# Fewer, larger DMAs in a two-layer attention kernel, and the DMAs that spread the sums of y moved from SyncE to ScalarE

## The reference

```
x = x + attn_a(layernorm(x))     # 16 heads of 16, causal softmax, then weights times a decay table of lag (0 from lag 511 on)
x = x + ffn(layernorm(x))        # 256 -> 1024 -> 256, weights alpha * sign(w), exact gelu
x = x + attn_b(layernorm(x))     # 16 heads of 16, causal softmax, biases, layernorm with gamma and beta behind it
x = x + ffn(layernorm(x))
```

## Time and profile before

| | |
|---|---|
| median of 3 runs | 2720.69 us (2717.49 to 2722.33) |
| the profiled execution's own time | 2716.31 us |
| its span, first to last instruction | 2714.6 us |
| mean granted TensorE clock | 0.947 |
| busy: PE / DVE / ACT / POOL | 2399.4 / 1956.2 / 1497.6 / 1054.6 us |
| first DMA of qkv_a, att_a, mid, att_b, end (SP) | at 34.3, 157.4, 1155.3, 1499.9, 2462.6 us |

### The profile page before, as it was taken

The page is one execution under the profiler, slowest core; times in us unless marked ns, Lnnn a source line. Parts: engine busy times, 40 slices in busy tenths (PEclk is TensorE's granted clock), DMA queues, the critical chain, the costliest instruction groups (busy, mean ns, idle before and its releaser), DMA issues. The chain is left out here.

```text
span 2714.6 us, 44575 instructions
## 1 busy us (share of the span) xinstructions
PE 2399.4 (88%) x13600; PEld 1368.4 (50%) x13600; DVE 1956.2 (72%) x4832; ACT 1497.6 (55%) x3293; POOL 1054.6 (39%) x1274
## 2 busy tenths in 40 slices
PE   4959999999999999749996699999999999993788
PEld 2535545555554555337764355555555555542666
DVE  5568888878887877337663787878788787842887
ACT  1218687776867767514331166666666666671233
POOL 0037877788787778713211301010000101003552
PEclk8969999999999999969998699999999999996999
DMA  4995142342514230055546742351523425004210
GB/s 129 254 144 70 22 61 40 45 53 30 78 26 56 40 45 6 8 151 116 118 96 127 92 63 39 44 68 28 66 35 49 62 30 69 8 5 136 70 55 32
DMA packets 185947, 180.66 MB, mean 67 GB/s; under 512 B 90352, under 2 KB 122864, under 8 KB 184944
## 3 DMA queue, kind: packets, MB, share of 16 engines
q1 hardware_dynamic: 185712, 177.81, 37.6%
HBM read 114.37 MB, written 61.60 MB: 65 GB/s over the span
## 5 line engine op out<-in xcount | busy, mean ns | idle before, releaser
L703 POOL TENSOR_TENSOR att_a_wd<-att_a_wt,decay 128x256 f32<-128x256 f32 (+3 forms) x896 | 754.7, 876 | 212.8 <-PE att_a_po L874 122.4
L729 ACT ACTIVATE att_b_wt<-att_b_ps 128x512 f32<-128x512 f32 (+3 forms) x1280 | 591.8, 538 | 347.6 <-PE att_b_ps L852 345.5
L769 DVE TENSOR_REDUCE att_a_mpart<-att_a_pm 128x1 f32<-128x512 f32 x768 | 508.6, 685 | 117.1 <-PE att_a_pm L839 112.5
L769 DVE TENSOR_REDUCE att_b_mpart<-att_b_pm 128x1 f32<-128x512 f32 x768 | 502.6, 684 | 96.2 <-PE att_b_pm L839 94.7
L839 PE MATMUL att_a_pm<-att_a_kop,att_a_qop 128*128 128x512 f32 (+3 forms) x1280 | 511.9, 425 | 54.2 <-DMA att_a_qop<-att_a_qop 28.9
L729 ACT ACTIVATE att_a_wt<-att_a_ps 128x512 f32<-128x512 f32 (+3 forms) x896 | 432.4, 510 | 210.7 <-PE att_a_ps L855 148.0
L839 PE MATMUL att_b_pm<-att_b_kop,att_b_qop 128*128 128x512 f32 (+3 forms) x1280 | 487.7, 399 | 49.8 <-DMA att_b_qop<-att_b_qop 30.6
L852 PE MATMUL att_b_ps<-att_b_qop,att_b_kop 128*128 128x512 f32 (+3 forms) x1280 | 455.3, 385 | 13.0 <-DMA att_b_qop<-att_b_mrow 8.2
L713 POOL TENSOR_SCALAR_AFFINE_SELECT att_b_wt<-att_b_wt 128x512 f32<-128x512 f32 x128 | 81.6, 637 | 851.0 <-ACT att_b_wt L729 851.0
L839 PEld LDWEIGHTS att_a_pm<-att_a_kop,att_a_qop 128*128 128x128 f32 x1280 | 238.8, 194 | 317.4 <-DVE att_a_mpart L769 140.3
L839 PEld LDWEIGHTS att_b_pm<-att_b_kop,att_b_qop 128*128 128x128 f32 x1280 | 245.0, 194 | 267.8 <-DVE att_b_mpart L769 131.4
(11 more groups left out here) (165 smaller groups left out, 2500.6 us busy)
## 6 DMA issues: line engine op xcount, KB each, us to landing
att_a_kop<-qk SPq DMA_DIRECT2D x128, 128.0 KB, 6.4
att_a_qop<-qk SPq DMA_DIRECT2D x128, 128.0 KB, 7.0
att_b_kop<-qk SPq DMA_DIRECT2D x128, 128.0 KB, 6.3
att_b_qop<-qk SPq DMA_DIRECT2D x128, 128.0 KB, 6.7
qk<-qkv_a_qk_hi SPq DMA_DIRECT2D x32, 256.0 KB, 4.8
qk<-qkv_a_qk_lo SPq DMA_DIRECT2D x32, 256.0 KB, 4.5
qk<-mid_qk_hi SPq DMA_DIRECT2D x32, 256.0 KB, 4.2
qk<-mid_qk_lo SPq DMA_DIRECT2D x32, 256.0 KB, 4.6
```

The source lines that it names most:

```text
L703: pool.tensor_tensor(wd[:, kq % 2, j, a:z], wt[:, kq % buffers, j, a:z], keep["decay"][:, u:u + z - a], ALU.mult).then_inc(w_decayed, 1)
L729: act.activation(wt[:, kq % buffers, j, a:CH], pe_[:, n % EBANKS, 0:CH - a], ACT.Exp)\
L769: dve.tensor_reduce(mpart[:, c, piece, u:u + 1], pm[:, n % MBANKS, 0:w], AX.X, ALU.max, negate=True).then_inc(m_reduced, 1)
```

## The change

1. Stores of q and k: the DRAM tensor `qk` is laid out so that one DMA stores all of hi and one all of lo, in `projections` and in "mid" (2 DMAs in place of 8), and hi is stored without a wait for lo. `v` is laid out so that one DMA stores all heads (1 in place of 4); the attention loads v of a group with 4 DMAs, one per chunk, in pieces of 256 or 272 bytes, in place of one with pieces of four times that.
2. Attention, the sums: `y` is stored whole, all 128 partitions, by one DMA of 256 KB in place of 4 of 32 KB. The 4 DMAs that spread the sums are begun by ACT, which first waits for its own copy (`o_kept`) and for `s_ready` of the chunk two before. `scol`, `inverse`, `mneg` and `ftotal` use every second column or partition of 32, so that the transposed far sums `frow` are added directly and the 8 DMAs of "FT" with `fcol` are gone.
3. Attention, the start: ACT begins the 16 `qop` loads of group 0, SP the 16 `kop` loads. Groups 0 and 1 have no DMA that clears the row of `qop`.
4. Dense: `load_y` begins 4 DMAs of 256 KB (two for y, two for inverse) in place of 17. At the start ACT begins wp, x of chunk 0 and the sign matrices; bo, gamma and beta have a semaphore of their own; the wait for the q, k, v weights on DVE stands ahead of item ("X", 1).

```diff
-                sp.wait_ge(hi_ready, M * G + M)
-                sp.wait_ge(lo_ready, M * G + 2 * M)
-                for hl, t in ((0, qk_hi), (1, qk_lo)):
-                    for a in range(2):
-
-                        for qk in range(2):
-                            dst = dram["qk"][b, :, hl, qk, :, c * CH:(c + 1) * CH]
-                            dst = dst.rearrange("(m a) p t -> a p m t", a=2)[a]
-                            sp.dma_start(dst, t[64 * a:64 * a + 64, par, KT * qk:KT * qk + KT, :].bitcast(F32))\
-                              .then_inc(stored[par], 16)
+                for hl, t, ready, n in ((0, qk_hi, hi_ready, M * G + M), (1, qk_lo, lo_ready, M * G + 2 * M)):
+                    sp.wait_ge(ready, n)
+                    dst = dram["qk"][b, hl].rearrange("q (m a) p t -> (a p) (q m) t", a=2)
+                    sp.dma_start(dst[:, :, c * CH:(c + 1) * CH], t[:, par, :, :].bitcast(F32)).then_inc(stored[par], 16)
                 sp.wait_ge(v_kept, G + 2)
-                for gh in range(NG):
-                    sp.dma_start(dram["v"][b, gh, c][:, 0:TB * GH * VW].rearrange("p (t j e) -> p t j e", t=TB, j=GH),
-                                 vt[:, par, :, GH * gh:GH * gh + GH, :]).then_inc(stored[par], 16)
+                sp.dma_start(dram["v"][b, c][:, 0:TB * H * VW].rearrange("p (t h e) -> p t h e", t=TB, h=H),
+                             vt[:, par, :, :, :]).then_inc(stored[par], 16)
...
+                    if g:
+                        sp.dma_start(qop[rows, par, c, :, :].bitcast(F32), qk_g[g][r // 2, 0, :, :, cols])\
+                          .then_inc(qk_in[par][c], 16)
                 if g < 2:
-                    sp.wait_ge(q_padded[par], c + 1)
-                sp.dma_start(qop[MROW:MROW + 1, par, c, :, :].bitcast(F32),
-                             qop[96:97, par, c, :, :].bitcast(F32)).then_inc(qk_in[par][c], 16)
-                if c == NC - 1:
-                    sp.dma_start(va[:, par, :, :, :].rearrange("p (c t) j e -> p c (t j e)", c=NC), v_g[g])\
-                      .then_inc(v_in[par], 16)
+                    sp.sem_inc(qk_in[par][c], 16)
+                else:
+                    sp.dma_start(qop[MROW:MROW + 1, par, c, :, :].bitcast(F32),
+                                 qop[96:97, par, c, :, :].bitcast(F32)).then_inc(qk_in[par][c], 16)
+                for a in range(NC) if c == NC - 1 else ():
+                    sp.dma_start(va[:, par, TB * a:TB * (a + 1), :, :], v_g[g][a]).then_inc(v_in[par], 16)
...
                 if kind == "O":
                     c = item[2]
                     sp.wait_ge(o_kept, done(g, c) + 1)
-                    if done(g, c) > 2:
-                        sp.wait_ge(s_ready, done(g, c) - 2)
-                    for j in range(GH):
-                        h, cols = GH * (g % NG) + j, slice(c * CH, (c + 1) * CH)
-                        sp.dma_start(dram["y"][g // NG, h, :, cols], y[STRIP * j:STRIP * j + HD, c % 2, :])\
-                          .then_inc(y_out[c % 2], 16)
-                        sums = y[STRIP * j + HD:STRIP * j + HD + 1, c % 2, :].rearrange("o (i e) -> o i e", e=PIECE)
-                        sp.dma_start(scol[STRIP * j:STRIP * (j + 1), c % 2, :], sums).then_inc(s_in[c % 2], 16)
+                    sp.dma_start(dram["y"][g // NG, g % NG, :, c * CH:(c + 1) * CH], y[:, c % 2, :])\
+                      .then_inc(y_out[c % 2], 16)
...
         @block.scalar
         def _(act):
+            for c in range(NC):
+                for r in range(PAIRS):
+                    act.dma_start(qop[r * HD:(r + 1) * HD, 0, c, :, :].bitcast(F32),
+                                  qk_g[0][r // 2, 0, :, :, c * CH:(c + 1) * CH]).then_inc(qk_in[0][c], 16)
...
                     act.activation(y[:, c % 2, :], po[:, :], ACT.Copy).then_inc(o_kept, 1)
+                    act.wait_ge(o_kept, done(g, c) + 1)
+                    if done(g, c) > 2:
+                        act.wait_ge(s_ready, done(g, c) - 2)
+                    else:
+                        act.wait_ge(m_padded, 2)
+                    sums = y[HD:P:STRIP, c % 2, :].rearrange("j (t k i) -> j k t i", t=TB, k=P // SQUARE)
+                    for k in range(P // SQUARE):
+                        act.dma_start(scol[SQUARE * k:SQUARE * (k + 1):SPREAD, c % 2, :], sums[:, k, :, :])\
+                           .then_inc(s_in[c % 2], 16)
...
-                        dve.wait_ge(f_in[n], F_DMAS * (g + 1))
-                        dve.tensor_tensor(scol[:, c % 2, :], scol[:, c % 2, :], fcol[:, n, :], ALU.add).then_inc(s_summed, 1)
+                        dve.wait_ge(f_turned, TURNED[g, c])
+                        dve.tensor_tensor(scol[:, c % 2, :], scol[:, c % 2, :], frow[:, n, :], ALU.add).then_inc(s_summed, 1)
...
-                sp.dma_start(y[:, G % 2, :, :], dram["y"][b].rearrange("(k h) d t -> (h d) k t", k=KT)[:, :, cols])\
-                  .then_inc(y_in[G % 2], 16)
-                for h in range(H):
-                    part = slice(HD * (h % (H // KT)), HD * (h % (H // KT) + 1))
-                    sp.dma_start(inverse[part, G % 2, h // (H // KT), :],
-                                 dram["inverse"][b, h // GH, c, h % GH:h % GH + 1, :].to_broadcast([HD, CH])).then_inc(y_in[G % 2], 16)
+                rows = dram["y"][b].rearrange("g (j s) t -> (g j) s t", s=STRIP)
+                for k in range(KT):
+                    heads = slice(k * H // KT, (k + 1) * H // KT)
+                    sp.dma_start(y[:, G % 2, k, :], rows[heads, 0:HD, cols]).then_inc(y_in[G % 2], 16)
+                    sp.dma_start(inverse[:, G % 2, k, :],
+                                 dram["inverse"][b, c, heads, :].unsqueeze(1).to_broadcast([H // KT, HD, CH]))\
+                      .then_inc(y_in[G % 2], 16)
...
             load_y(0)
-            sp.dma_start(wp[:, :, :], w.rearrange("(t p) n -> p t n", p=P)).then_inc(w_in, 16)
-            load_x(0)
             if norm:
                 for t, src in zip((bo, gamma, beta), norm):
-                    sp.dma_start(t[:, :], row_of(src).to_broadcast([P, D])).then_inc(w_in, 16)
-            sp.dma_start(w1s[:, :, :].bitcast(F32), dram["w1s"]).then_inc(signs_in, 16)
-            sp.dma_start(w2s[:, :, :].bitcast(F32), dram["w2s"]).then_inc(signs_in, 16)
+                    sp.dma_start(t[:, :], row_of(src).to_broadcast([P, D])).then_inc(norm_in, 16)
             load_y(1)
...
+            act.dma_start(wp[:, :, :], w.rearrange("(t p) n -> p t n", p=P)).then_inc(w_in, 16)
+            act.dma_start(x[:, 0, :, :], at(x_src, 0, 0)).then_inc(x_in[0], 16)
+            act.dma_start(w1s[:, :, :].bitcast(F32), dram["w1s"]).then_inc(signs_in, 16)
+            act.dma_start(w2s[:, :, :].bitcast(F32), dram["w2s"]).then_inc(signs_in, 16)
...
-            if qkv:
-                dve.wait_ge(qkv_in, N_QKV)
-                dve.tensor_scalar(bqk[:, 0:KT], bqk[:, 0:KT], SCALE, None, ALU.mult)
-                dve.tensor_scalar(wqkv[:, :, 0:D], wqkv[:, :, 0:D], SCALE, None, ALU.mult).then_inc(w_scaled, 1)
-                dve.wait_ge(w_scaled, 1)
-                dve.wait_ge(vt_filled, 2)
-
             for item in PLAN:
                 G = item[1]
                 par = G % 2
+                if item == ("X", 1) and qkv:
+                    dve.wait_ge(qkv_in, N_QKV)
+                    dve.tensor_scalar(bqk[:, 0:KT], bqk[:, 0:KT], SCALE, None, ALU.mult)
+                    dve.tensor_scalar(wqkv[:, :, 0:D], wqkv[:, :, 0:D], SCALE, None, ALU.mult).then_inc(w_scaled, 1)
+                    dve.wait_ge(w_scaled, 1)
+                    dve.wait_ge(vt_filled, 2)
```

More of the change, by code:

```diff
@@ L554, in attention @@
             ftotal, frow = sb("ftotal", [P, NC - 2, SQUARE], F32), sb("frow", [P, NC - 2, SQUARE], F32)
-            fcol = sb("fcol", [P, NC - 2, PIECE], F32)
         y = sb("y", [P, 2, CH], F32)
-        scol, inverse = sb("scol", [P, 2, PIECE], F32), sb("inverse", [P, 2, PIECE], F32)
+        scol, inverse = sb("scol", [P, 2, SQUARE], F32), sb("inverse", [P, 2, SQUARE], F32)
         pm, pe_, po = ps("pm", [P, MBANKS, CH]), ps("ps", [P, EBANKS, CH]), ps("po", [P, CH])
@@ L575, in attention @@
         block = ctx.enter_context(nc.Block())
-        qk_g = dram["qk"].rearrange("b g h q (j d) t -> (b g) h q d j t", d=HD)
-        v_g = dram["v"].rearrange("b g c p e -> (b g) p c e")[:, :, :, 0:TB * GH * VW]
+        qk_g = dram["qk"].rearrange("b h q g (j d) t -> b g h q d j t", d=HD)
+        qk_g = [qk_g[g // NG, g % NG] for g in range(GROUPS)]
+        v_g = [[dram["v"][g // NG, c][:, 0:TB * H * VW].rearrange("p (t g e) -> g p t e", t=TB, g=NG)[g % NG]
+                .rearrange("p t (j e) -> p t j e", j=GH) for c in range(NC)] for g in range(GROUPS)]
         KBS = sum(len(near(c, decayed)) for c in range(NC))
@@ L656, in _ @@
                     for k in range(P // SQUARE):
-                        sp.dma_start(row[:, :, k, :], mrow[SQUARE * k:SQUARE * k + UNITS, c, :].bitcast(F32))\
```

(21 more changed lines are left out.)

64 lines of the change are left out of this document (28 added, 36 removed).

## The result

The changed kernel takes 2799.09 us (median of 4 runs, 2791.84 to 2803.77) where the kernel before takes 2720.65 (4 runs): the ratio is 1.0287 with a 95% interval of 1.0258 to 1.0317. It is slower, as forecast, but by 78 us and not by 18, and it lies above the range that was given.

A forecast was written before the change was run, and what follows sets the result against it. PE was taken to bound both attention stages. Gains of 60 us against 78 us of PE waits behind ACT's issues gave 18 us slower, 2734.3 for an execution like the profiled one, median 2739; range 2690 to 2775.

The forecast's parts named there:

- The loss: Both attentions: ACT stands about 2.2 us issuing DMAs at each O, PE waits 1.25 us per item, 78 us.
- rival C: Attentions: an occasional full queue or a PE clock dropping after stalls costs another 0.5 us per item, 2770; chance 0.08.
- Rival A: Attentions: ACT's stall is partly absorbed or its issues are shorter, so the kernel is faster, 2700 or 2671; chance 0.29.
- qkv_a, chunks and end: First projection: fewer SP issues save 2 us over 7 chunks, and att_a begins 3.5 us earlier.
- first load to first M, two attentions: Attention starts: the ninth DMA, which clears a row behind the others, goes; 2.5 us each, 5 us.
- ends of the attentions: Last spreading DMA begins some 2 us earlier, with four on ACT instead of eight on SP: 4 us for both.
- start of mid: No wait for `bv`; y, inverse and ACT's loads all arrive in 9.5 us, so PE starts 15.5 us earlier.
- mid after its first P: End of mid: with merged stores att_b begins at 1493.9 instead of 1499.9, 6 us.
- start of end: Same load sum as in mid gives a PE start at 2476 against 2478.95, 3 us.
- waits in att_b: Waits for `scol` and the row of maxima both go, 19 us, plus 2 us for lower clock: 21 us.
- Projections: qkv_a and mid: merged stores save 2 us in chunks, 3.5 us before att_a and 6 us before att_b.
- rival D: Dense starts: y loads with 8 heads outermost use half the DMA engines, 3 us each, 2745; chance 0.05.

The follow-up runs named there:

- e1: Changed kernel, but SyncE begins the four spreading DMAs again, behind its store of y: 2676.32 us, ratio 0.984.
- e4: Changed kernel, but ScalarE begins the four spreading DMAs one at a time, one behind each of its next four exponentials: 2677.8 us.
- e3: Changed kernel, but each of ScalarE's four spreading DMAs is cut in two, eight issues in a row: 3002.5 us.
- e2: Changed kernel, but ScalarE begins two of the four spreading DMAs and SyncE the other two: 2710.0 us.
- e10: e1 with the stores of qk and v cut into twelve DMAs a chunk again, in the new layouts: 2687.14 us, ratio 0.9892.
- e5: e1 with wp, x and the sign matrices begun by SyncE behind y, inverse and three rows, ahead of the second chunk's loads: 2666.1 us, ratio 0.9811.
- e11: e5 with y in its old DRAM layout, loaded by one DMA over 128 rows and stored by four at each O: 2665.1 us, ratio 0.9812.
- e9: e5 with the first chunk's y on SyncE and inverse on ScalarE, 8 DMAs each of outer dimension 16: 2671.7 us, ratio 0.9834.

## Why the prediction was right and wrong

The losses were sized at 78 us and measured at 125.9 (span of after less that of e1); the gains at 60 and measured at 38.5 (before less e1). The net is 87.4 us between the profiled executions, where 18 were forecast.

**The loss.** The mechanism was right: ACT's standstill, the banks, PE behind them in both stages, and nothing for it in att_a or att_b's slack. Its waits were sized right too: 1.23 us per item (76 us in all) against 1.25, behind a standstill of 2.38 us in the middle of the items against 2.2. The step that failed is that these waits were the whole loss. The PE clock was held at no loss, since it stood near 1.00 in steady groups with short waits, and matmuls that take longer behind a stall were in no term. They take 48 us longer in the two stages, 0.77 us per item, so that the loss is 2.00 us per item (1.98 by the medians) where 1.25 was forecast. The clock can have at most 43 of the 48 us; the rest stays open. A falling clock was one half of rival C, which got 0.08 and 0.5 us per item. Its other half, a queue that is now and then full, showed little: the longest issue in att_b is 0.59 us, and in att_a 3 of 128 are above 0.7 (1.27 the longest). So of the 69 us between forecast and result 48 are the longer matmuls, and 21.5 the gains that did not come.

The Trainium skill, page "DMA: Bandwidth & Descriptors", section "Issuing engines are not separate DMA queues", holds that spreading DMAs over engines saves only sequencer time, usually small beside the DMA itself. By e4 (1.5 us for all) that is so where the sequencer has room; by e3 (326 us) it is not, where an engine that feeds PE through three banks issues them in a row.

**Rival A** turned on a loss of 0.97 us per item, at a block of 1.9 us. On the line between e2 (1.25 us of block, 0.54 lost) and after (2.38, 1.98) that loss stands at 1.6 us. With gains of 38.5 us in place of 60 the sign turns at 0.62 us per item; e2 lies just below, and is just faster than before (2710.0 us, ratio 0.997, 0.9953 to 0.9986).

**The gains, one by one** (before against e1, and the same rows of e1):

| term | forecast | measured |
|---|---|---|
| qkv_a, chunks and end | 5.5 | 10.2 |
| first load to first M, two attentions | 5 | 3.9 |
| ends of the attentions | 4 | 2.9 |
| start of mid | 15.5 | 9.0 |
| mid after its first P | 6 | 8.9 |
| start of end | 3 | -3.2 |
| waits in att_b | 21 | 10.0 |
| att_a, end after its first P | 0 | -3.2 |

*Projections* were undersized: SP's issues, about half of the gain by e10, had held them back, and the bytes less than was taken. The last v is issued at 142.3 in e1 against 149.84 to 153.4, and its last 9.2 us move 284 GB/s at a share of 0.72, where 264 at a share of 1.01 had been taken for a limit of the engines.

*Starts of mid and end* were oversized by one step: "all 3.75 MB are in 9.5 us". The 395 GB/s of the earlier trace rows were the best of one stretch; in e1 the nine windows of 2 us from 1144 to 1162 move 151 to 348 GB/s. And y did not share the time evenly: it was complete last, 18.9 us after the first load. e5 puts the contention with ScalarE's 2.75 MB and SyncE's second chunk at 8.7 and 7.9 us for the two starts. e11 puts rival D at 2.2 and 2.1 us for the product, near its 2.5, with y alone changed and inverse still in 8 heads. The Trainium skill, the same page, section "Why a DMA increments its semaphore by 16 and not by 1", has 8 engines for an outer dimension of 8; the share of 0.62 in e5, where a half would be 0.50, agrees roughly. So the wait for `bv` did go, and half of the gain at mid went to a new wait; in end, where before loaded wp and the signs behind y, the change made the start slower.

*Waits in att_b* were oversized: DVE's waits for `scol` fell, and PE's behind it, but the wait for the row of maxima stayed, 6.6 us in 6 waits in e1 where before had 5.6 in 6. "MC's DMAs queue behind O's eight on SP" holds in a way: the DMAs of 13 of the 32 rows in before began 0.7 to 2.2 us behind their transposition. But PE waited for none of these. The 8 rows that it waited for began at once, as this one of before:

```profile
1613.74 0.21 DVE L809 STREAM_TRANSPOSE att_b_mrow<-att_b_mneg 128x32 f32<-128x32 f32 x1
1613.97 2.44 SPq L657 DMA_DIRECT2D att_b_qop<-att_b_mrow  x4
1617.60 0.50 PE L852 MATMUL att_b_ps<-att_b_qop,att_b_kop 128*128 128x512 f32 x1 [0.93 <-DMA att_b_qop<-att_b_mrow]
```

In e1 it is the same. The row's DMAs begin straight behind the transposition at 1690.94 (DVE and SP of e1), and the S matmul starts at 1694.82: the row's own 3.7 us are what PE waits for.

```profile
1690.94 0.20 DVE L799 STREAM_TRANSPOSE att_b_mrow<-att_b_mneg 128x32 f32<-128x32 f32 x1
...
1691.17 2.49 SPq L652 DMA_DIRECT2D att_b_qop<-att_b_mrow  x4
```

```profile
1694.82 0.50 PE L842 MATMUL att_b_ps<-att_b_qop,att_b_kop 128*128 128x512 f32 x1 [0.95 <-DMA att_b_qop<-att_b_mrow]
```

## What to carry to other kernels

A DMA that ScalarE or SyncE begins here holds its order of work for half a microsecond; ask what that engine feeds and how long its buffers last, and put issues one by one between its instructions rather than in a row: the same four cost 123 us in a row and 1.5 us one by one. Where a change makes PE stand, count the slower matmuls behind the stall too, here nearly two thirds of the wait again. At the start of a stage begin what the first instruction needs first and alone; in this kernel a second queue for later data held it up by some 8 us. And look at many places before you size a step: the item with the plainest picture here was the longest of its stage.

## What the runs showed of the hardware that was not expected

- The first two issues in a row cost the kernel 0.27 us each and those beyond the second 0.7 to 0.8, more than their length of 0.53.
- The granted clock fell to 0.50 within 8 us of the copy at 1 of 62 items with two issues in a row (e2), at 19 with four (after) and at 61 with eight (e3).
- An issue of ScalarE's runs beside its own exponential: of 0.53 us, 0.44 or less is seen as idle time (e4).
- DMAs of 16 partitions each showed a share of 1.14 at 159 GB/s (e9); 8 heads over 128 partitions moved 172 GB/s at a share of 0.62 (e5), and y over 128 rows with inverse in 8 heads 263 GB/s at 0.75 (e11).
